# A four-layer decoder on one core: value rows in two arrangements, the third block's weights kept twice, and another order of work in a slot

## What is computed

```
qkv = shift_tokens(x) @ Wqkv                  # 16 heads of 64
q = l2norm(q) * qs ; k = l2norm(k) * ksc      # then a rotation by position, with a scale
out = local_attention(q, k, v)                # windows of 32 tokens; a window sees itself and the one before
x = x + out @ Wo
xn = layernorm(shift_tokens(x)) * g + bln
a, gate = split(xn @ W1 + b1)
x = x + (a * gelu(gate)) @ W2 + b2
```

## Time and profile before

| | us |
|---|---|
| median of 3 runs | 5369.28 |
| lowest, highest | 5364.82, 5372.76 |
| the profiled execution, its own time | 5376.34 |
| its span in the profile | 5374.4 |

### The profile page before, as it was taken

The page is one execution under the profiler, slowest core; times in us unless marked ns, Lnnn a source line. Parts: engine busy times, 40 slices in busy tenths (PEclk is TensorE's granted clock), DMA queues, the critical chain, the costliest instruction groups (busy, mean ns, idle before and its releaser), DMA issues. The chain is left out here.

```text
span 5374.4 us, 115360 instructions
## 1 busy us (share of the span) xinstructions
PE 4459.1 (83%) x45624; PEld 2769.2 (52%) x45624; DVE 3578.9 (67%) x6837; ACT 2725.0 (51%) x4622; POOL 2494.3 (46%) x2314
## 2 busy tenths in 40 slices
PE   7768999999999999777863888887798869985779
PEld 5555666666666666524641343433365444423445
DVE  4347777777777777466446999999855526646646
ACT  3325666666666666463323566565465415542322
POOL 8426666666666666343054666666633310001100
PEclk8779999999999999877856999999999959996889
DMA  1001111111111111000000000000000000003000
GB/s 23 16 21 34 30 49 34 46 34 42 38 44 40 30 30 34 17 0 2 2 11 14 1 1 0 1 0 1 3 13 1 1 18 5 16 1 74 5 21 7
DMA packets 110461, 102.56 MB, mean 19 GB/s; under 512 B 37143, under 2 KB 80424, under 8 KB 109160
## 3 DMA queue, kind: packets, MB, share of 16 engines
q1 hardware_dynamic: 107879, 94.14, 7.1%
q0 software_dynamic: 2048, 1.05, 0.1%
HBM read 40.18 MB, written 1.18 MB: 8 GB/s over the span
## 5 line engine op out<-in xcount | busy, mean ns | idle before, releaser
L4201 POOL TENSOR_TENSOR l_attn_read<-l_attn_state,l_attn_c_rows 128x1024 f32<-128x1024 f32 x256 | 605.0, 2364 | 291.0 <-DVE l_attn_state L4103 173.0
L2999 POOL TENSOR_TENSOR l_ffn_t<-l_ffn_t 128x512 f32<-128x512 f32 x384 | 488.3, 1272 | 506.5 <-DVE l_ffn_t L2866 506.5
L2597 PE MATMUL psum<-l_ffn_wq,l_ffn_xsT 128*128 128x512 f32 x1152 | 601.8, 614 | 97.9 <-DVE l_ffn_t L2866 96.5
L3823 PE MATMUL psum<-l_attn_read,ident 128*128 128x512 f32 x1024 | 491.5, 598 | 7.3 <-DVE l_attn_yz L4111 5.0
L3005 POOL TENSOR_TENSOR l_ffn_t<-l_ffn_t,l_ffn_ss 128x512 f32<-128x512 f32 x384 | 401.1, 1045 | 0.7 <-DVE l_ffn_ss L2881 0.7
L2862 DVE TENSOR_TENSOR l_ffn_t<-psum,l_ffn_tab 128x512 f32<-128x512 f32 x384 | 258.8, 674 | 121.9 <-ACT l_ffn_sq L2748 119.2
L4103 DVE TENSOR_TENSOR_SCAN l_attn_state<-l_attn_decay,psum 128x1024 f32<-128x1024 f32 x144 | 329.0, 2284 | 4.5
L2645 PEld LDWEIGHTS psum<-l_ffn_pT,l_ffn_v 64*64 64x64 f32 x3072 | 248.9, 135 | 142.9 <-issue 138.8
L2597 PEld LDWEIGHTS psum<-l_ffn_wq,l_ffn_xsT 128*128 128x128 f32 x1152 | 180.0, 191 | 274.3 <-DVE l_ffn_t L2866 237.7
L3979 ACT ACTIVATE l_attn_decay<-l_attn_dt,l_attn_a 128x1016 f32<-128x1016 f32 x256 | 292.9, 1144 | 36.0 <-DVE l_attn_state L4100 32.6
L2645 PE MATMUL psum<-l_ffn_pT,l_ffn_v 64*64 64x64 f32 (+1 forms) x3072 | 306.1, 227 | 1.1 <-ACT l_ffn_pT L2764 1.1
(11 more groups left out here) (914 smaller groups left out, 11451.6 us busy)
## 6 DMA issues: line engine op xcount, KB each, us to landing
l_ffn_vx<-l_ffn_v SPq DMA_DIRECT2D x192, 128.0 KB
l_ffn_vx<-l_ffn_v SPq DMA_DIRECT2D x384, 64.0 KB
l_ffn_wq<-in_L_ffn_Wqkv SPq DMA_DIRECT2D x6, 1536.0 KB, 6.4
l_xattn_toep<-s4d_taps SPq DMA_DIRECT2D x4, 2048.0 KB, 17.2
l_ffn_wo<-in_L_ffn_Wo SPq DMA_DIRECT2D x6, 512.0 KB, 3.6
l_ffn_w<-in_L_ffn_W SPq DMA_DIRECT2D x6, 341.0 KB
l_ffn_w<-in_L_ffn_w SPq DMA_DIRECT2D x3, 512.0 KB, 4.1
x_all<-in_x SPq DMA_DIRECT2D x4, 256.0 KB, 4.4
```

The costliest lines, as they stand in the source:

```text
L2597: nc.tensor.matmul(ring[it % 2], xsT[:, n % 2, m % G, :], w, start=True, stop=True).then_inc(itemed, 1)
L2999: nc.gpsimd.tensor_tensor(t1[:, m % G, i, :], t1[:, m % G, i, :], t2[:, x % 3, :], ALU.add).then_inc(added, 1)
L3823: last = nc.tensor.matmul(total[:, h * GT:(h + 1) * GT], K.ident[:], read[:, k % 3, h * GT:(h + 1) * GT], start=(n == 0), stop=(n == N - 1 ...
L4201: nc.gpsimd.tensor_tensor(read[:, k % 3, :].rearrange("p (h n) -> p h n", h=2), state[:, k % 3, :].rearrange("p (h n) -> p h n", h=2), row ...
```

## The change

It has three parts.

1. **Values.** The transposed weights are copied into a wider `pT` of five windows of columns per head pair instead of four: the third window stands twice, once multiplied by a column `keep` that is 1 on partitions of windows 0 and 2 and 0 elsewhere, once by its counterpart. The value product is then two products (96 and 64 columns) instead of three (64, 32, 32), the second adding to what the first wrote, and the mixed arrangement and four of the six transfers are gone. `move_p` becomes three ScalarE instructions instead of one.
2. **Order.** In every slot the projection comes first on TensorE and its square first on ScalarE; the value items move behind `turn_item`. VectorE rotates before it takes the maximum, and adds the output projection at the start of the next slot. The exponential moves behind the copy of a turned item. The feed-forward part is spread otherwise: moments in slot 6, transposition in 10, gates in 11, 13 and 14, GELU in 15, the other half in slots 0, 1 and 2 of the next step, down projection in slot 3. Half of the shifted rows is no longer made by TensorE and ScalarE but copied by GpSimd (`unshifted_in`). The network's weights of the next layer are fetched in slot 4 instead of 1.
3. **Taps.** In the first block GpSimd makes no taps ahead of the first group's norm, then three, three and two.

```diff
@@ taps, on GpSimd in small_heads
                     if local and g:
-                        s4d.taps(pool, 2 * g)
-                        s4d.taps(pool, 2 * g + 1)
-                    if local and g == 0:
-                        s4d.taps(pool, 0)
-                        s4d.taps(pool, 1)
+                        for a in range(3 * (g - 1), min(3 * g, s4d.HI)):
+                            s4d.taps(pool, a)
@@ misc_at
+        GATE_AT = (11, 13, 14)
...
-                if u == 8:
+                if u == 10:
                     return ("ht", n)
-                if u in (9, 10, 11):
-                    return ("g", n, u - 9)
-                if u in (13, 14, 15):
-                    return ("a", n, u - 13)
-            if u == 0 and 0 <= n - 1 < NSTEP:
-                return ("w2", n - 1)
+                if u in GATE_AT:
+                    return ("g", n, GATE_AT.index(u))
+            if 0 <= n - 1 < NSTEP:
+                if u < 3:
+                    return ("a", n - 1, u)
+                if u == 3:
+                    return ("w2", n - 1)
@@ value, on TensorE
                     for i in range(4):
-                        for at, n, kinds in ((0, 2 * W, (own[0], far)), (2 * W, W, (mixed, mixed)), (3 * W, W, (far, own[1]))):
+                        for to, at, n, kinds in ((0, 0, 3 * W, (own[0], far)), (2 * W, 3 * W, 2 * W, (far, own[1]))):
...
-                    nc.tensor.matmul(ps[:, :, 0:64], K.ident[:], r_all[:, q * G:(q + 1) * G, 0:64], start=True, stop=True)
@@ TensorE's loop
+                    if tau < NSTEP:
+                        project(4 * tau + u // 4, u % 4)
                     if k % 2 == 0 and 0 <= k // 2 < NU:
                         score(k // 2)
                     if k % 2 == 0 and 0 <= k // 2 - 1 < NU:
                         turn_p(k // 2 - 1)
-                    if tau < NSTEP:
-                        for i in items_at(u % 4):
-                            project(4 * tau + u // 4, i)
                     if k % 2 == 1 and 0 <= (k - 3) // 2 < NU:
                         value((k - 3) // 2)
                     if turn_at(tau, u) is not None:
                         turn_item(*turn_at(tau, u))
+                    if tau < NSTEP and u % 2 == 1:
+                        project(4 * tau + u // 4, 4 + u % 4 // 2)
@@ move_p, on ScalarE
-                    nc.scalar.copy(pT[:], TP.rearrange("p (h t) -> p h t", h=4)).then_inc(pt_moved, 1)
...
+                    nc.scalar.activation(to[:, :, 0:4:3, :], blocks[:, :, 0:3:2, :], ACT.Identity, scale=keep[:, 0:1])
+                    nc.scalar.activation(to[:, :, 2, :], blocks[:, :, 2, :], ACT.Identity, scale=keep[:, 1:2])
+                    nc.scalar.copy(to[:, :, 1:5:3, :], blocks[:, :, 1:4:2, :]).then_inc(pt_moved, 1)
@@ unshifted_in, new on GpSimd in slot 5
+                        wait_moved(pool, "op", 4 * n + i)
+                    nc.gpsimd.tensor_copy(xs[:, :, 0:64], r_all[:, n % NG * G:n % NG * G + G, 0:64]).then_inc(half_in, 1)
```

More of the change, by code:

```diff
@@ L2634, in value @@
                     m, c = k // 2, k % 2
-                    own, far, mixed = [v[:, m % NV, par, :, :] for par in range(2)], vx[:, m % 2, 0, :, :], vx[:, m % 2, 1, :, :]
+                    own, far = [v[:, m % NV, par, :, :] for par in range(2)], vx[:, m % 2, :, :]
                     pe.wait_ge(pt_moved, k + 1)
                     if c == 0:
-                        pe.wait_ge(spread[m % 2], 16 * 6 * (m // 2 + 1))
+                        pe.wait_ge(spread[m % 2], 16 * 2 * (m // 2 + 1))
                     if k >= 1:
@@ L2787, in shifted_in @@
                         act.wait_ge(filled, use["ht", n - 1] + 1)
-                    done(nc.scalar.copy(xs[:].rearrange("p g d -> p (g d)"), take("sh", n)), "sh", n)
+                    done(nc.scalar.copy(xs[:, :, 64:128], take("sh", n).rearrange("p (g d) -> p g d", g=G)[:, :, 64:128]), "sh", n)
                 def norm(n):
@@ L2827, in _ @@
                         move_turn(*turn_at(tau, u))
+                    if k % 2 == 0 and 0 <= k // 2 < NU:
+                        exp(k // 2)
                     if tau < NSTEP and u % 2 == 1:
@@ L2962, in _ @@
                     n = tau - 2
-                    if k % 2 == 0 and 0 <= k // 2 < NU:
-                        peak(k // 2)
+                    before = (tau, u - 1) if u else (tau - 1, 15)
+                    if out_at(*before) is not None:
+                        add_out(out_at(*before))
                     if k % 2 == 1 and 0 <= k // 2 < NU:
@@ L3022, in rstd_, with unshifted_in @@
                     nc.gpsimd.tensor_tensor(nb[:], nb[:], rs[:], ALU.mult).then_inc(rstd_ready, 1)
+                def unshifted_in(n):
+                    if n:
+                        pool.wait_ge(filled, use["ht", n - 1] + 1)
+                    for i in range(G):
+                        wait_moved(pool, "op", 4 * n + i)
+                    nc.gpsimd.tensor_copy(xs[:, :, 0:64], r_all[:, n % NG * G:n % NG * G + G, 0:64]).then_inc(half_in, 1)
                 def add_b2(n):
@@ L3054, in _ @@
                                               pattern=[[-1, T]], channel_multiplier=1))
+                const(nc.gpsimd.memset(keep[:], 0.0))
+                for at in range(0, 4):
+                    const(nc.gpsimd.memset(keep[W * at:W * at + W, at % 2:at % 2 + 1], 1.0))
                 for tau, u in slots:
```

66 lines of the change are left out of this document (35 added, 31 removed).

## The result

| | before | after |
|---|---|---|
| median, us (5 runs each; before, with the three of the section above) | 5366.68 | 5337.00 |
| lowest, highest | 5364.82, 5372.76 | 5330.31, 5347.56 |
| profiled execution | 5376.34 | 5330.66 |
| first block | 205.3 | 187.2 |
| third block | 1883.1 | 1867.3 |

The ratio of the medians' runs is 0.9944, 95% interval 0.9925 to 0.9963: the changed kernel is 0.6% faster, 30 us where 3 were forecast. The time lies inside the range, but outside the forecast case's own 5355 to 5379. (Blocks run between the starts of the instruction that drains TensorE's queue at each block's end; the step is the mean of the first 20 distances between two add_down.)

What follows compares the result with a forecast made beforehand. TensorE was taken as busiest, its waits coming from a ScalarE and VectorE chain; 68.3 us of issues plus 8.3 of waits made a 76.6 us step. First block -23 and third +20 gave 5366 us, range 5305 to 5405.

Steps and rivals of the forecast that it cites:

- forecast case: Whole kernel: first block -23 us, third block +20 us, giving 5366 us (5355 to 5379); chance 0.36.
- the two bad places: Third block, pairs of slots 8-9 and 0-1: ScalarE's square 3.1 us behind its projection, TensorE waiting 4.0 and 3.1 us.
- the three copies: ScalarE's copies of the transposed weights: 1.03 us together (0.95 to 1.5), costing nothing while under 1.1.
- the lead and the value product together: TensorE, each pair of slots: about 0.19 us ahead of the value product, then the product itself at 1.20 us.
- the wait at x_all: First block: ScalarE's 20.63 us wait for GpSimd's two taps ahead of the first norm would go.
- The slower rival of the copies: Third block: at 1.5 us the weights' copies delay each value product 0.45 us, 40 us in all, 5406; chance 0.18.
- The rival that four wider pairs of passes take as long as six: Value product: nothing saved by the wider form, 28 us come back, 5394; chance 0.12.
- invert, 1.46 us: VectorE's chain in slots 8-9 and 0-1: invert counted at 1.46 us, read from the old trace (1228.60 to 1230.06).
- Value product, 0.32 saved: TensorE, third block: fewer, wider passes save 0.32 us per unit, 2.6 a step.
- Ends of the block: Third block, steps 1 and 24: they carry fewer parts and gain some 2 us.
- First block, -23: First block: 20.6 us of ScalarE's wait and 2.5 of TensorE's clock given back, -23 us (-20 to -25).
- the faster rival: Third block: one of the two bad places does not arise, time 5321 us (5290 to 5355); chance 0.34.

## Why the prediction missed its size

The measured time lies in the forecast's range, but the forecast case itself put the third block at +20 us and it came at -16. Its path was right and one term was too large.

**Right: the path, its pairs and the places.** What bounds a step, the two bad places, their cause (ScalarE 3.1 us behind its projection: measured 3.13 and 3.36), the three copies (0.99 us for 1.03), the lead and the value product together (1.37 us for 1.39), the wait at x_all. The slower rival of the copies did not arise: the value product waits for them only in slot 9 of each step, 0.6 us. The rival that four wider pairs of passes take as long as six fell with the runs on values.

**Wrong term: invert, 1.46 us.** It stands in both bad places, in the step "length 0.61, invert 0.60 and 1.46". The trace has 0.68. The 1.46 was read off without asking what stood beside it. The 0.95 in it were 0.18 of work and a wait for the end of GpSimd's addition, which the new order itself takes away: it puts maximum and subtraction between rotation and invert, and the addition is over by then. Twice 0.78 is 1.56 a step: 76.6 becomes 75.0, against 75.17 measured. That is 34 us in 22 steps, and the sign of the third block with it (+20 becomes -14; measured -16). The run that puts the addition back beside it shows the 0.95; it gives the price in the other direction only together with the 0.72 us of the exponential, which length and invert no longer cover there. The run with invert ahead of the length gives it alone: 0.95 becomes 0.18 and the step 1.0 us shorter.

**Value product, 0.32 saved.** Measured 0.25 (1.52 to 1.27). Two pairs of heads start 0.28 us apart where 0.27 was worked out from columns; the rest of the difference, 0.03, stands behind the last. The estimate by the Trainium skill's 60 cycles for every product (page TensorEngine Tiling (Array Packing), section Instruction Overhead) was 0.16. The measured 0.25 lies halfway between the two. In the new order it is worth 0.75 a step, in the old 1.4.

**Ends of the block.** Steps 1 and 24 were put at -2. The later first add_down costs 12 us and the shorter last three distances give 19: -7.

**First block, -23.** Measured -18 in the kernel after, -23 with the taps alone, -19 in the medians. The wait is gone, but its 20.6 us were those of one execution (17.9 and 16.7 in two others with the same code), and in the kernel after ScalarE reached x_all at 96.04, not at the forecast's 93.35.

**Sum.** Measured, the two blocks give 34 us on the profiled execution; the medians give 30. That 5337 lies in the faster rival's 5290 to 5355 is luck: both bad places arose and ScalarE was no earlier at them; about 0.8 us went from each by another cause.

**Missed: the parts against each other.** The forecast put +1.0 us a step on the whole change. Without the new order the step is 74.3, so the order, with root and norm where the change puts them, costs 0.9 and hides most of the 1.4 that the values give. The prediction laid out the new order by pairs and never the old order with the new values, so it could not see this.

## What to carry to other kernels

Before a duration from a trace enters a sum, look at what ran beside it: here a small VectorE instruction that ended with a GpSimd instruction, wherever it had started, was waiting for it, and moving it by 0.6 us was worth more than its whole length. What a saving on the busiest engine was worth followed the stretches that this engine bounds, not its busy share or its wait in total. Cost each part of a change alone as well as the whole, since a part that loses can hide behind one that gains.

## What the runs showed of the hardware

- A tensor_scalar and a tensor_tensor of 128x64 from SBUF to SBUF on VectorE take 0.18 and 0.22 us alone, and 0.95 and 0.99 when they start 0.36 us into an addition of 1.27 us on GpSimd: they end 0.04 to 0.08 us behind it. Started 0.08 us into it, the tensor_scalar takes 1.24. The reciprocal (0.55) and the sums of squares (0.67) are not held up. A tensor_scalar that starts 0.23 us ahead of the addition takes 0.18 and the addition its 1.27.
- In the middle of work at the full granted clock, TensorE's clock fell to its lower level (1.2 GHz, 0.50 in the stretch) behind a wait of 2.36 us in one step and not behind 2.37 us in the next; it fell in every step behind 3.75, in 3 of 19 behind two waits of some 1.6 and 1.0 us close together in that same kernel, and in none of the kernel after's behind 2.19. It cost 1.4 us in most steps, and 2.8 in 2 of 19 behind the 3.75: a wait is then dearer than its length.
- A table load on ScalarE took 1.28 us everywhere. A square and a copy behind GELU's, the root's or the exponential's table needed no load of their own.
